# Moving the first split of the second product's operand ahead of the last early weight chunk

## The reference, cut to what matters

```python
adj = adjacent_mat((A + A.T) * 0.5)
y = Coefficient2 @ adj        # Coefficient2 is adj too
y = y @ x
```

```python
scale = clip(mean(abs(W), axis=-1), 1e-5)
w_q = clip(round(W / scale), -1, 1) * scale
```

## Time and profile before

| | |
|---|---|
| median of 3 runs | 705.63 us (699.36, 705.63, 707.70) |
| the profiled execution | 702.86 us |
| its span, first to last instruction | 701.2 us |
| PE busy | 648.4 us, 92% |
| DVE busy | 469.2 us, 67% |
| ACT busy | 389.6 us, 56% |
| PE clock granted, mean | 0.991 |
| last matmul group of the first product to the first of the second | from 201.97 to 206.89 us |

### The profile page before, as it was taken

One profiled execution on the slowest core, in us unless ns is written; L12 is line 12 of the kernel. 1 busy time (PEld: TensorE's weight loads), 2 busy tenths in 40 slices (PEclk: granted clock), 3 DMA queues, 4 the chain that ended last, 5 costly groups with the idle time before them and its releaser, 6 DMA issues.

```text
span 701.2 us, 15954 instructions
## 1 busy us (share of the span) xinstructions
PE 648.4 (92%) x5281; PEld 381.6 (54%) x5281; DVE 469.2 (67%) x1031; ACT 389.6 (56%) x726; POOL 151.7 (22%) x171
## 2 busy tenths in 40 slices
PE   0798999999979999999998789999999999999995
PEld 0343444444434554445434367777767677777773
DVE  4878988566664555688788669756855565555553
ACT  1658648879986776777657653333432242424241
POOL 2234430000000000012323206200021353434322
PEclk9999999999999999999999999999999999999999
DMA  8999962675897777866576896643284876868641
GB/s 348 417 421 417 421 255 62 194 196 155 237 242 251 264 259 253 282 225 237 175 270 218 241 248 166 173 111 96 76 141 131 197 195 176 187 185 181 177 141 31
DMA packets 107103, 151.68 MB, mean 216 GB/s; under 512 B 64286, under 2 KB 64286, under 8 KB 102944
## 3 DMA queue, kind: packets, MB, share of 16 engines
q1 hardware_dynamic: 91280, 117.74, 53.5%
q0 software_dynamic: 6960, 20.99, 9.9%
q10 hardware_dynamic: 8800, 12.09, 5.7%
HBM read 119.57 MB, written 19.16 MB: 198 GB/s over the span
## 4 chain that ended last, share of the span: by engine, by line
PE 54%; DMA 14%; DVE 13%; ACT 9%; issue 7%; SPq 1%; POOL 1%; DVEq 0%; ACTq 0%; POOLq 0%
PE bank L1545 16%; PE bank L1517 16%; PE bank L1390 7%; PE bank L1392 7%; PE bank L1391 7%; DMA region<-in_adj_t 6%; ACT junk L748 4%; DMA work<-in_w 3%; ACT region L760 2%; DVE work L1096 2%; DVE region L986 2%; PE bank L1421 2%; DMA work<-in_adj_t 1%; DVE region L1192 1%; DVE region L982 1%
## 5 line engine op out<-in xcount | busy, mean ns | idle before, releaser
L1545 PE MATMUL bank<-region,work 128*128 (+1 forms) x624 | 141.6, 379 | 4.4 <-DVE work L1244 4.2
L886 ACT ACTIVATE work<-work 128x512 f32<-128x512 f32 x78 | 48.5, 622 | 171.1 <-DVE work L1234 171.1
L1390 PE MATMUL bank<-zreg,work 128*128 (+1 forms) x256 | 98.2, 384 | 12.3 <-DVE work L1164 10.9
L1517 PE MATMUL bank<-zreg,region 128*128 128x128 f16 x1728 | 100.9, 219 | 0.0
L1517 PEld LDWEIGHTS bank<-zreg,region 128*128 (+1 forms) x1728 | 98.1, 98 | 4.2
L1391 PE MATMUL bank<-zreg,work 128*128 (+1 forms) x256 | 98.2, 384 | 0.0
L1392 PE MATMUL bank<-zreg,work 128*128 (+1 forms) x256 | 98.0, 383 | 0.0
L1390 PE MATMUL bank<-region,work 128*128 128x512 f16 x192 | 74.1, 386 | 25.4 <-DVE region L1010 25.4
L1545 PEld LDWEIGHTS bank<-region,work 128*128 128x128 f16 x624 | 58.9, 98 | 70.4 <-issue 7.4
L748 ACT ACTIVATE junk<-work 128x512 f16<-128x512 f32 x124 | 77.6, 625 | 15.9 <-DMA work<-in_w 13.8
L1244 DVE SCALAR_TENSOR_TENSOR work<-work 128x512 f16<-128x512 f32 x78 | 53.7, 691 | 48.8 <-ACT work L893 48.8
(11 more groups left out here) (154 smaller groups left out, 946.8 us busy)
## 6 DMA issues: line engine op xcount, KB each, us to landing
work<-in_w SPq DMA_DIRECT2D x62, 512.0 KB, 4.1
region<-in_adj SPq DMA_DIRECT2D x16, 1024.0 KB, 10.7
region<-in_adj_t SPq DMA_DIRECT2D x16, 1024.0 KB, 7.5
work<-in_adj_t SPq DMA_DIRECT2D x32, 384.0 KB, 4.4
zreg<-s_scratch SPq DMA_DIRECT2D x24, 256.0 KB, 3.9
xb<-in_w SPq DMA_DIRECT2D x10, 512.0 KB, 4.2
zreg<-in_x SPq DMA_DIRECT2D x4, 1024.0 KB, 9.7
h_scratch<-hb POOLq DMA_DIRECT2D x16, 256.0 KB, 3.4
```

The costliest lines, as they stand in the source:

```text
L886: nc.scalar.activation(h1[:, cols], pre[:, cols], ACT.Silu).then_inc(h1_ok, 1)
L1390: nc.tensor.matmul(dst, a_hi, b_hi, start=start, stop=False, skip_group_check=True)
L1517: last = nc.tensor.matmul(ps_h[b][f // 4][:, (f % 4) * P:(f % 4 + 1) * P], w, ht[n % RING][:, c:c + P], start=(f % 4 == 0 and d == 0 and h ...
L1545: last = nc.tensor.matmul(ps_y[b][:, :].rearrange("p (d c) -> p d c", d=DB), h1hl[:, b, h, f * P:(f + 1) * P], w, start=(f == 0 and h == 0 ...
```

## The change

Nothing is added or removed; instructions trade places on three engines. On ACT, `high(0,0)`, the four `z_high` and `high(0,1)` move ahead of the store of chunk 25 and of the sums of chunk 27. On DVE, `low(0,0)`, the four `z_low` and `low(0,1)` move ahead of the ternary of chunk 27, and the r steps stand behind that ternary as before. On SP, the turn of chunk 27 moves from step 1 to step 2, so behind the load of chunk 29 and block 2. PE's list is the same.

```diff
--- before.py
+++ after.py
@@ -446,8 +446,8 @@
                     sp.dma_start(at_end[:, j % 3, :] if g == 2 else at[:, s % 2, 0:nc_],
                                  adjt_j[ds(j, 1), :, c0:c0 + nc_].rearrange("a p n -> (a p) n")
                                  ).then_inc(at_end_loaded[j % 3] if g == 2 else at_loaded[s % 2], 16)
-                    if isinstance(m, int) and m == 0 and s < 2:
-                        turn(EARLY_CHUNKS - 3 + 2 * s)
+                    if isinstance(m, int) and m == 0 and s in (0, 2):
+                        turn(EARLY_CHUNKS - 3 + s)
                     if not (isinstance(m, int) and m == IDLE):
                         load_w(later(g, m - (g == 2), s), s % 2)
                 if g == 0:
@@ -767,6 +767,10 @@
 
             LAG = 3
 
+            def early_sums(q):
+                act.wait_ge(early_loaded[q % 3], 16 * (q // 3) + 16)
+                sums(early_at(q), q % 2, raw_early[q % 3], q < 2)
+
             def early_round(rnd):
                 for s in range(ROUND_STEPS):
                     k = ROUND_STEPS * rnd + s + 2
@@ -778,8 +782,8 @@
                     if q >= LAG:
                         store_w(early(rnd, s - LAG) if s >= LAG else early(rnd - 1, s - LAG + early_count(rnd - 1)),
                                 (q - LAG) % 2)
-                    act.wait_ge(early_loaded[q % 3], 16 * (q // 3) + 16)
-                    sums(early(rnd, s), q % 2, raw_early[q % 3], q < 2)
+                    if q < EARLY_CHUNKS - 1:
+                        early_sums(q)
 
             early_round(0)
             early_round(1)
@@ -849,11 +853,12 @@
                     act.dma_start(s2_rows[k, c0:c1, :], s2t[32 * k + c0 - base:32 * k + c1 - base, :]
                                   ).then_inc(s2_stored[part], 16)
 
-            store_w(early(ROUNDS - 1, early_count(ROUNDS - 1) - LAG), (EARLY_CHUNKS - LAG) % 2)
             act.wait_ge(rest_step, 2 * NT - 3)
             high(0, 0, 0, True)
             z_high(2)
             high(0, 1, 1, True)
+            store_w(early(ROUNDS - 1, early_count(ROUNDS - 1) - LAG), (EARLY_CHUNKS - LAG) % 2)
+            early_sums(EARLY_CHUNKS - 1)
             macro(0, 0, True)
             store_s2(0, EARLY0, CHUNKS, S2_FROM[0])
             with act.Fori(1, 4) as m:
@@ -1107,7 +1112,8 @@
                         part_low(k)
                     if s < early_count(rnd):
                         q = early(rnd, s)[0]
-                        ternary(early(rnd, s), q % 2, raw_early[q % 3], q < 2)
+                        if q < EARLY_CHUNKS - 1:
+                            ternary(early(rnd, s), q % 2, raw_early[q % 3], q < 2)
 
             part_low(0)
             part_low(1)
@@ -1198,17 +1204,17 @@
                 r_n[0] += 1
                 chained(ins, r_seq, r_n[0])
 
+            low(0, 0, 0)
+            z_low(2)
+            low(0, 1, 1)
+            last = EARLY_CHUNKS - 1
+            ternary(early_at(last), last % 2, raw_early[last % 3])
             dve.wait_ge(small_in, 48)
             rstep(nc.vector.tensor_copy(r3[:, :, 0, :], rt[:, :, :]))
             rstep(nc.vector.tensor_tensor(rtr[:, :, :], rt[:, :, :], r3[:, :, 0, :], ALU.subtract))
             rstep(nc.vector.tensor_copy(r3[:, :, 1, :], rtr[:, :, :]))
             rstep(nc.vector.tensor_tensor(rtr[:, :, :], rtr[:, :, :], r3[:, :, 1, :], ALU.subtract))
             nc.vector.tensor_copy(r3[:, :, 2, :], rtr[:, :, :]).then_inc(r3_ok, 1)
-
-            dve.wait_ge(small_in, 48)
-            low(0, 0, 0)
-            z_low(2)
-            low(0, 1, 1)
             macro(0, 0)
             turn_s2(0, EARLY_CHUNKS)
             with dve.Fori(1, 4) as m:
```

## The result

| | before | changed |
|---|---|---|
| median of 16 runs, us | 703.01 (699.24 to 707.70) | 707.03 (703.24 to 710.31) |
| profiled execution, us | 702.86 | 707.23 |
| its span, us | 701.2 | 705.6 |
| ratio to before, 95% interval | | 1.0053 (1.0032 to 1.0075) |

The changed kernel is 0.53% slower, about 3.7 us of 703.0 (2.2 to 5.3 by the interval). The forecast was 707.9 us, a rise of 3.6 from an assumed 704.25; the measured level of the kernel before is 703.01.

The account below looks back on a forecast made before the run. PE was taken as the bound, decided by when chunk 31's transposes start. Step 0's -1.85 is used up, +0.9 at chunk 28 covered, +3.6 from loads 29 and 31 carried through: 704.25 to 707.9 us, range 702.5 to 713.0.

Parts of the forecast that it names:

- Step 0 earlier, no further than block 0 lets it: PE's first matmul of the second product starts at 205.05, 1.85 us earlier, held by block 0's landing at 203.1.
- Transposes of 28 at 213.4 after a pause of 2.7 to 4.4 us: On PE, chunk 28's transposes wait for its ternary and start at 213.4 against 212.47, 0.9 us late.
- Load 29 at 211.1, landing in 4.3 us: On SP, chunk 29's load waits for ternary 27, goes out near 211.1 instead of 206.25 and lands at 215.4.
- Sums of 31 near 222.3 after a wait for load 31: On ACT, chunk 31's sums start when its load lands at 222.3 instead of at 218.72, 3.6 us late.
- chain over the loads of 29 and 31: Ternary 27 releases load 29, ternary 29 releases load 31, the sums of 31 follow: +3.6 us, carried to the end.
- Transposes of 31 at 229.4, 3.6 us late: On PE, chunk 31's transposes start at 229.4 instead of 225.84, an unchanged 7.1 us after the sums of 31.
- Carried through to the end: PE is busy 51.50 of 51.50 us from 226.5 to 278.0, so a delay there reaches the end in full.
- a distance to the end more than a microsecond off 475.4 us: Sign of being wrong, measured from the transposes of 31; it would mean slack behind 226 not found.
- The clock drops out: PE's 1.7 us at 1.2 GHz would now end inside 2.1 us of slack; counted at one chance in four.
- inside step 0, which the end followed: In the kernel before, the half-rate clock's 1.7 us lay in PE's step 0 and was followed by the end.
- The early start: Rival at the transposes of 28: PE keeps 1.85 us and perhaps 1.7 of clock, -3.5, 700.7 us; chance 0.08.
- The collision: Rival: load 29, block 2, turn 27, load 30 and block 3 slow each other from 211 to 214, +7.2; chance 0.18.

Follow-up runs that it names:

- run 4: Changed kernel with the five router steps on DVE moved behind the ternary of 29; ratio to before 1.0045.
- run 6: Changed kernel with block 1's high(0,1) and low(0,1) moved behind chunk 27's store, sums and ternary; ratio to before 1.0052.
- run 3: Changed kernel with loads 28 and 29 released one count earlier, by the chunk whose buffer they take; ratio to before 1.0020.
- run 8: Changed kernel with block 1 behind chunk 27, router steps behind ternary 29, loads 28 and 29 released by their buffers; ratio to before 1.0006.
- run 11: Kernel before with 60 unused transposes of the identity in PE's pause ahead of step 0; ratio to before 0.9970.
- run 9: Changed kernel with loads 28 and 29 released by their buffers and router steps behind ternary 29, block 1 left in front; ratio to before 1.0007.
- run 5: Kernel before with loads 28 and 29 released one count earlier, by the chunk that used their buffer; ratio to before 1.0003.
- run 7: Kernel before with high(0,0) and z_high ahead of the store of 25, router steps behind ternary 29, loads 28 and 29 released by their buffers; ratio 0.9993.
- run 10: Kernel of run 8 with unused transposes on PE, 30 ahead of step 0 and 40 ahead of the transposes of 28; ratio to before 1.0006.
- run 12: Kernel of run 7 with 60 unused transposes in PE's pause; ratio to the kernel before 0.9990.
- run 2: Changed kernel with SP's turn of chunk 27 put back in front of the load of 29; ratio to before 1.0044.

## Why the prediction was right

- *Step 0 earlier, no further than block 0 lets it.* Forecast 205.05, measured 204.56. Block 0 landed in 6.2 us, not 7.0, in an execution in which all of this lies 0.3 us later. The gain was spent by the next wait, as forecast.
- *Transposes of 28 at 213.4 after a pause of 2.7 to 4.4 us.* Measured 212.97 after 2.66, released by line 1101. In the chain, the router steps were counted at their full microsecond; run 4 showed 0.5, since the sums of 28 come just behind.
- *Load 29 at 211.1, landing in 4.3 us.* Measured 210.70 and 3.8. The transfer in front of the turn was not slowed by it; what came behind, load 30, took 5.9. The prediction set against this the ring order of the Trainium skill ("DMA: Bandwidth & Descriptors", "Queues, rings and completion order"), by which each DMA engine takes descriptors in the order of the ring; load 29's 3.8 us agree with it. Block 0, with a turn issued 2.4 us behind it, again took longer, 6.2 us, and no run shows whether the turn has a part in that.
- *Sums of 31 near 222.3 after a wait for load 31.* The time was right, 221.87, the cause only in part. The step that failed is the last link of "chain over the loads of 29 and 31", that the sums of 31 wait for load 31: this load went out at 217.81, right behind ternary 29 as forecast, but had landed at 221.4, and the sums of 31 followed the sums of 30, which had waited for load 30, released by ternary 28 and slowed by the crowd. The prediction gave load 30 no price. By its own chain the sums of 31 would have started near 221.4, 2.7 us late instead of 3.2, so half a microsecond of the agreement is luck. The two chains, over 29 and 31 and over 28 and 30, end that close together; in runs 4 and 6 the chain over load 31 came last, by 0.2 and 0.1 us. Run 3 takes away the first and the crowd of the second at once, so it cannot divide the 2.3 us between them; a faster load 30 alone would have gained 0.5 us at most, since load 31 stood behind it. The hold of ternary 29 by the turn (0.47 us) was not counted either.
- *Transposes of 31 at 229.4, 3.6 us late.* Measured 228.90, 3.1 late. The time rose by 3.7 us by the ratio. "Carried through to the end" holds as far as the traces can show it, 124 us behind the mark. The prediction named as a sign of being wrong a distance to the end more than a microsecond off 475.4 us. It was 476.7, so this sign was met, but it was drawn too tight: the same stretch varies by 6.9 us, and a single profile can't show slack of this size.
- *The clock drops out.* In the changed kernel it did: step 0 at 0.50, none behind the mark. In other versions it fell into step 1; it reached the mark in run 8, but not in run 4. That before it was "inside step 0, which the end followed" is not shown: run 11's times leave room for it, its trace does not show it.
- *The rivals.* The early start was not kept. The collision was there in part: load 30 took 5.9 us and came last, but the delay at the mark was 3.1 us, not 7.2.

## What to carry to other kernels

An instruction moved forward in a list written by hand pushes back every count that the overtaken one gives; look up who waits for that count and what is queued behind those waits. Here the steps moved forward gained 2.3 us for one matmul group and held back the ternaries that release the next transfers, which cost 3.7 us in all. A wait one count too careful, free in the old order, accounts for about 2.3 of these; with it and five small steps moved out of the way the cost is gone (run 9). Where PE is busy for a long stretch behind a place, only the time at which it becomes busy there counts. And where two chains end within half a microsecond, shortening one shows next to nothing (run 4).

## What the runs showed of the hardware

The same load ahead of the second product (chunk 27, 512 KB) landed 5.0 to 7.3 us after its issue and block 0 5.7 to 8.0 us, from one execution to the next, while load 30 with little beside it took 3.7 and 3.8 us in runs 3 and 8. (In runs 3, 5, 7 to 10 and 12 the load of 28 follows closer behind and may add to this; without these the ranges are 5.0 to 6.5 and 5.7 to 7.2.) After pauses of 2 to 5 us PE's clock fell to the 1.2 GHz level, but not always in the step right behind the pause. Step 0 ran partly at that level in nine of the eleven kernels without added transposes, after pauses of 1.98 us (run 3) to 4.92 (before); in runs 4 and 8 it did not (1.86 and 2.51 us), and step 1 did instead, after 4.35 and 3.19 us. In run 2 both steps did (3.00 and 2.49 us), while in the changed kernel and in runs 3, 6 and 9 step 1 ran at full clock behind pauses of 2.66, 3.10, 2.47 and 1.75 us. So the length of the pause alone does not say where the low level falls. With 60 transposes of no use in PE's longest pause step 0 ran at full clock both times (runs 11 and 12); the time fell by 0.3% (0.1 to 0.5) in the first and by nothing that shows in the second.
